# Six result buffers, x accumulated by DMA and the linear part on GpSimd in the spline stage of a convolution and spline kernel

## The reference

```python
out = relu(batchnorm(conv3x3(x, sign(w1)), gamma1, beta1))
out = batchnorm(conv3x3(out, sign(w2)), gamma2, beta2)
x = relu(out + x)                                   # input of the spline
u = (clip(a * x + b, -1.5, 1.5) + 1.0) * 0.5 * (K - 1)   # K = 32 cells
i = floor(u); t = clip(u - i, 0, 1)
i0, i1, i2, i3 = clip(i - 1), clip(i), clip(i + 1), clip(i + 2)      # to 0..K-1
spline = alpha[i0]*b0(t) + alpha[i1]*b1(t) + alpha[i2]*b2(t) + alpha[i3]*b3(t)   # cubic, R = 8
y_nl = einsum('bchwr,cr->bchw', spline, mix)
return id_gain * x + y_nl + bias
```

## Time and profile before

| | us |
|---|---|
| time before, median of 3 runs | 1254.49 (1253.94 to 1254.75) |
| the profiled execution, own time | 1254.66 |
| its span, first to last instruction | 1252.8 |
| first convolution and its norm | about 0 to 214 |
| second convolution and its norm | about 214 to 424 |
| spline, 32 chunks | 427 to 1253 |
| busy over the span | PE 1058.6, DVE 1062.8, ACT 868.8, POOL 113.4 |
| mean granted clock of PE | 0.926 of full speed |

### The profile page before, as it was taken

One profiled execution on the slowest core, in us unless ns is written; L12 is line 12 of the kernel. 1 busy time (PEld: TensorE's weight loads), 2 busy tenths in 40 slices (PEclk: granted clock), 3 DMA queues, 4 the chain that ended last, 5 costly groups with the idle time before them and its releaser, 6 DMA issues. The chain is left out here.

```text
span 1252.8 us, 51454 instructions
## 1 busy us (share of the span) xinstructions
PE 1058.6 (85%) x23562; PEld 710.2 (57%) x23562; DVE 1062.8 (85%) x951; ACT 868.8 (69%) x424; POOL 113.4 (9%) x189
## 2 busy tenths in 40 slices
PE   6999996999999368887888788878887888788876
PEld 4688885788888234554545455444544545455444
DVE  5765656766666689999999999999999999999987
ACT  4454544777787267688868877887788778877881
POOL 6000000282000000000000000000000000000000
PEclk9999998999999778998989889898998989889898
DMA  7666766576777386677767766777677667776552
GB/s 227 259 257 256 276 255 225 217 277 252 271 264 300 136 235 181 183 216 194 185 189 213 196 181 193 208 192 184 189 214 192 184 197 206 194 182 197 157 114 78
DMA packets 58215, 260.85 MB, mean 208 GB/s; under 512 B 16336, under 2 KB 16336, under 8 KB 50000
## 3 DMA queue, kind: packets, MB, share of 16 engines
q1 hardware_dynamic: 52528, 230.88, 56.3%
q0 software_dynamic: 4608, 25.69, 11.0%
q10 hardware_dynamic: 928, 1.90, 0.6%
HBM read 104.29 MB, written 77.07 MB: 145 GB/s over the span
## 5 line engine op out<-in xcount | busy, mean ns | idle before, releaser
L1181 PE MATMUL tab<-edge_mask,diag 128*32 128x392 bf16 x10240 | 501.8, 358 | 132.6 <-DVE poly L1090 130.8
L1181 PEld LDWEIGHTS tab<-edge_mask,diag 128*32 128x32 f16 x10240 | 281.7, 104 | 339.0 <-DVE poly L1090 143.4
L982 ACT ACTIVATE edge_mask<-cell,thr 128x6272 bf16<-128x6272 bf16 x62 | 338.5, 5508 | 0.0
L711 PE MATMUL acc<-split,w 64*64 64x392 f16 x4608 | 195.9, 329 | 12.0 <-DVE w L463 10.8
L711 PE MATMUL acc<-band_split,w 64*64 64x392 f16 x4608 | 197.9, 330 | 9.4 <-ACT band_split L368 7.2
L410 ACT ACTIVATE yout<-acc 128x1568 f32<-128x1568 f32 x64 | 94.2, 1473 | 160.6 <-PE acc L711 139.4
L1181 PE MATMUL tab<-middle_mask,diag 128*32 128x392 bf16 x4096 | 183.4, 332 | 25.0 <-DVE middle_mask L1052 25.0
L711 PEld LDWEIGHTS acc<-band_split,w 64*64 64x64 f16 x4608 | 164.1, 107 | 42.9 <-issue 14.1
L711 PEld LDWEIGHTS acc<-split,w 64*64 64x64 f16 x4608 | 155.3, 107 | 51.9 <-issue 12.6
L520 DVE BATCH_NORM_STATS2 stats<-yout 128x392 f32 (+1 forms) x240 | 118.0, 555 | 60.2 <-ACT yout L410 59.4
L930 ACT ACTIVATE zbuf<-lin,cst 128x1568 f32<-128x1568 f32 x32 | 54.3, 1697 | 163.8 <-DVE lin L1016 157.9
(11 more groups left out here) (126 smaller groups left out, 816.9 us busy)
## 6 DMA issues: line engine op xcount, KB each, us to landing
y_scratch<-yout SPq DMA_DIRECT2D x32, 1568.0 KB, 6.2
cell<-cell SPq DMA_DIRECT2D x496, 98.0 KB, 3.3
xin<-y_scratch SPq DMA_DIRECT2D x16, 1568.0 KB, 9.0
zbuf<-y_scratch SPq DMA_DIRECT2D x32, 784.0 KB, 5.9
lin<-in_x SPq DMA_DIRECT2D x32, 784.0 KB, 6.1
lin<-far POOLq DMA_DIRECT2D x32, 784.0 KB, 8.8
out<-lin SPq DMA_DIRECT2D x31, 784.0 KB, 4.1
xin<-in_x SPq DMA_DIRECT2D x15, 1568.0 KB, 9.3
```

The lines of the kernel that those rows point to most:

```text
L711: mm = pe.matmul(acc[h * C:(h + 1) * C, 2 * k + r, 0:TILE], weights[part][own, tap * C:(tap + 1) * C], image[own, first:first + ROWS, dx:d ...
L982: act.activation(mask_of(b, q)[:, :, :], cell4[b % 2][:, :, :], ACT.Sign, bias=thr[:, q:q + 1]).then_inc(sign_mask_ready, 1)
L1181: mm = pe.matmul(tab[(b + t) % 2][j * GROUP:(j + 1) * GROUP, sub, 0:SUB], keep["diag"][part][:, j % 2, t, q, :], mask_of(b, q)[:, j, sub * ...
```

## The change

- `lin` has six buffers instead of four. SP loads y2 (not x) straight into `lin` (`load`), four chunks ahead; chunks 0 and 1 are still loaded as before, in the convolutions' last round.
- ACT multiplies y in place (`scale`), and POOL issues a DMA that accumulates x onto it (`add_x`). Both stand three chunks ahead. `position` waits for that DMA (`x_added`) instead of for `total`, which is left for chunks 0 and 1 only.
- `linear` moves from DVE to POOL. POOL's queue is now, for each chunk, `linear(c + 2)`, `add_x(c + 3)`, `add_far(c)`.
- DVE multiplies `poly` by the offset twice (`times_offset`, from the integers) in place of `near_part`, `slope` and `add_slope`: square table, times offset, linear table, times offset. `distance_square` and `dist_sq` are gone. Because `slope` no longer writes `far_sq`, ACT's `far_square` waits for `far_part` of the chunk before.
- `finish(c - 1)` stands after `near_cube(c)`, where it stood ahead of it. On SP `store(c - 1)` stands after `spread(c + 2)`, where it stood first.
- All spline programs are written out for 32 chunks, without a loop.
- SP no longer waits for y2's stores ahead of the barrier; it does so in the spline, ahead of `load(2)`. The first ACT instruction is a square root (of a constant) instead of a copy.

```diff
-BUFS = 4
+LIN = 6
...
-            for b in range(2):
-                sp.wait_ge(stored[b], 32 * half_rounds)
...
-            act.activation(tmp[:, 5:6], row_scale[:, 0:1], ACT.Identity)
+            act.activation(tmp[:, 5:6], row_scale[:, 0:1], ACT.Sqrt)
...
-                wait_past(sp, offset_ready, before)
-                wait_past(sp, cell_ready, before)
-                sp.dma_start(place[b % 2][:, :], ysrc).then_inc(y_loaded[b % 2], 16)
-                wait_past(sp, stored[b % BUFS], free)
-                sp.dma_start(lin[b % BUFS][:, :], xsrc).then_inc(x_loaded[b % BUFS], 16)
...
+            def load(c):
+                wait_past(sp, stored[c % LIN], 16 * (c // LIN))
+                sp.dma_start(lin_of(c)[:, :], image_half(y2, c)).then_inc(y_loaded[c % LIN], 16)
...
-            def body(i, b, n):
-                if exists(n, b - 1):
-                    store(i, b - 1)
-                if exists(n, b + 3):
-                    load(i, b + 3)
-                if exists(n, b + 2):
-                    spread(i, b + 2)
...
+            spread(0)
+            for b in range(2):
+                sp.wait_ge(keep["y_stored"][b], 16 * PAIRS)
+            load(2)
+            spread(1)
+            load(3)
+            for c in range(CHUNKS):
+                if c + 4 < CHUNKS:
+                    load(c + 4)
+                if c + 2 < CHUNKS:
+                    spread(c + 2)
+                if c > 0:
+                    store(c - 1)
...
+            def linear(c):
+                pool.wait_ge(place_ready, c + 1)
+                pool.tensor_scalar(lin_of(c)[:, :], lin_of(c)[:, :], cc(NEG_B2),
+                                   par[:, ID_GAIN:ID_GAIN + 1], ALU.max, ALU.mult).then_inc(lin_ready, 1)
...
+            def add_x(c):
+                pool.wait_ge(scaled, c - 1)
+                pool.dma_start(lin_of(c)[:, :], image_half(x, c), accum_op=ALU.add).then_inc(x_added, 16)
...
+            linear(0)
+            linear(1)
+            add_x(2)
             for c in range(CHUNKS):
+                if c + 2 < CHUNKS:
+                    linear(c + 2)
+                if c + 3 < CHUNKS:
+                    add_x(c + 3)
                 add_far(c)
...
+            def scale(c):
+                act.wait_ge(y_loaded[c % LIN], 16 * (c // LIN + 1))
+                act.activation(lin_of(c)[:, :], lin_of(c)[:, :], ACT.Identity, scale=cc(BN2_S)).then_inc(scaled, 1)
...
+            def position(c):
+                if c < 2:
+                    act.wait_ge(sum_ready, c + 1)
+                else:
+                    act.wait_ge(x_added, 16 * (c - 1))
+                    act.wait_ge(offset_ready, c - 1)
+                    act.wait_ge(cell_ready, c - 1)
+                act.activation(place[c % 2][:, :], lin_of(c)[:, :], ACT.Identity, bias=cc(U_B),
                                scale=cc(U_S)).then_inc(place_ready, 1)
...
-                wait_past(act, slope_ready, 2 * c)
+                wait_past(act, far_part_ready, c)
...
-                c = BUFS * i + b
-                act.wait_ge(offset_ready, c + 1)
-                wait_past(act, near_ready, 2 * c)
-                act.activation(dist_sq[:, :], offset[b % 2][:, :], ACT.Square,
-                               scale=1 / POINT).then_inc(dist_sq_ready, 1)
...
-            def body(i, b, n):
-                following, after = exists(n, b + 1), exists(n, b + 2)
-                far_distance(i, b)
-                if after:
-                    position(i, b + 2)
-                far_square(i, b)
-                if after:
-                    cells(i, b + 2)
-                distance_square(i, b)
-                if following:
-                    distance(i, b + 1)
-                    edge(i, b + 1, EDGE_QUADS[0])
-                if following:
-                    edge(i, b + 1, EDGE_QUADS[1])
...
+            for c in range(2):
+                position(c)
+                cells(c)
+                spread(c)
+            distance(0)
+            scale(2)
+            for c in range(CHUNKS):
+                far_distance(c)
+                if c + 2 < CHUNKS:
+                    position(c + 2)
+                if c + 3 < CHUNKS:
+                    scale(c + 3)
+                far_square(c)
+                if c + 2 < CHUNKS:
+                    cells(c + 2)
+                if c + 1 < CHUNKS:
+                    distance(c + 1)
+                    for q in EDGE_QUADS:
+                        edge(c + 1, q)
...
-            def linear(i, b):
-                dve.wait_ge(place_ready, BUFS * i + b + 1)
-                dve.tensor_scalar(lin[b % BUFS][:, :], lin[b % BUFS][:, :], cc(NEG_B2),
-                                  par[:, ID_GAIN:ID_GAIN + 1], ALU.max, ALU.mult).then_inc(lin_ready, 1)
...
-            def near_part(i, b):
-                c = BUFS * i + b
-                dve.wait_ge(table_used, used(i, b, T_SQ))
-                dve.wait_ge(dist_sq_ready, c + 1)
-                dve.tensor_tensor(poly[b % 2][:, :], poly[b % 2][:, :], dist_sq[:, :], ALU.mult).then_inc(near_ready, 2)
...
-            def slope(i, b):
-                c = BUFS * i + b
-                dve.wait_ge(far_part_ready, 2 * c + 2)
-                dve.wait_ge(table_ready, used(i, b, T_LIN))
-                dve.scalar_tensor_tensor(out=quarters(far_sq), in0=summed(i, b, T_LIN), scalar=base(i, b, T_LIN),
-                                         in1=quarters(offset[b % 2]), op0=ALU.add, op1=ALU.mult).then_inc(table_used, 1)
...
-            def add_slope(i, b):
-                c = BUFS * i + b
-                dve.wait_ge(table_used, used(i, b, T_LIN))
-                dve.wait_ge(near_ready, 2 * c + 2)
-                dve.scalar_tensor_tensor(out=poly[b % 2][:, :], in0=far_sq[:, :], scalar=1 / POINT,
-                                         in1=poly[b % 2][:, :], op0=ALU.mult, op1=ALU.add).then_inc(slope_ready, 2)
...
+            def times_offset(c, t, done):
+                dve.wait_ge(table_used, used(c, t))
+                dve.scalar_tensor_tensor(out=poly[c % 2][:, :], in0=offset[c % 2][:, :], scalar=1 / POINT,
+                                         in1=poly[c % 2][:, :], op0=ALU.mult, op1=ALU.mult).then_inc(done, 1)
...
-            def body(i, b, n):
-                previous, following, after = exists(n, b - 1), exists(n, b + 1), exists(n, b + 2)
-                if previous:
-                    add_table(i, b - 1, T_VAL, slope_ready, 2 * (BUFS * i + b - 1) + 2)
-                    finish(i, b - 1)
-                if after:
-                    total(i, b + 2)
-                near_cube(i, b)
-                if after:
-                    fixed(i, b + 2)
-                    linear(i, b + 2)
-                far_cube(i, b)
-                far_part(i, b)
-                if following:
+            for c in range(CHUNKS):
+                if c > 0:
+                    add_table(c - 1, T_VAL, slope_ready, c)
+                if c + 2 < CHUNKS:
+                    fixed(c + 2)
+                near_cube(c)
+                if c > 0:
+                    finish(c - 1)
+                far_cube(c)
+                far_part(c)
+                if c + 1 < CHUNKS:
                     for q in MIDDLE_QUADS:
-                        middle(i, b + 1, q)
-                add_table(i, b, T_SQ, table_used, used(i, b, T_NEAR))
-                near_part(i, b)
-                slope(i, b)
-                add_slope(i, b)
-                if after:
-                    offsets(i, b + 2)
-            rounds(dve, body)
+                        middle(c + 1, q)
+                add_table(c, T_SQ, table_used, used(c, T_NEAR))
+                times_offset(c, T_SQ, near_ready)
+                add_table(c, T_LIN, near_ready, c + 1)
+                times_offset(c, T_LIN, slope_ready)
+                if c + 2 < CHUNKS:
+                    offsets(c + 2)
```

269 lines of the change are left out of this document (110 added, 159 removed).

## The result

| | before | after |
|---|---|---|
| time, median of 4 runs | 1254.61 us (1253.94 to 1254.75) | 1288.22 us (1286.73 to 1291.67) |
| ratio, 95% interval | | 1.0273 (1.0252 to 1.0294) |
| the profiled execution, own time and span | 1254.66, 1252.8 | 1291.67, 1289.8 |
| first and last `far_cube` | 459.44, 1233.89 | 468.03, 1271.06 |
| one chunk, mean of 31 | 24.98 | 25.90 |

The forecast was 1230 us, with a range from 1222 to 1266: wrong in sign. The account of the two profiled executions closes: 31 x (25.90 - 24.98) = 28.6 us in the chunks, 8.6 in a later first `far_cube`, -0.2 behind the last one, together 37.0 us of span. Against the forecast it closes too: 31 x (25.90 - 24.0) = 59.0, 2.9 for the first `far_cube` and -0.2 for the end are the 61.7 us between 1230 and 1291.67.

What follows compares the result with a forecast made beforehand. DVE, 97% busy, looked like the bound, with a loop through PE almost as long that would bind next at 24.0 us a chunk. 1254.66 - 0.7 - 2.3 + 8.7 - 30.4 = 1230 us, range 1222 to 1266.

Steps and rivals of the forecast that it cites:

- the paragraph on POOL: POOL's queue: `linear` estimated at about 4.0 us, issued with both DMAs well ahead of `far_part`, costing nothing if undisturbed.
- Rival 1: POOL's `linear` holds up DVE's `fixed`: cadence 24.8, total 1255 us, from 1246 to 1283; chance 0.34.
- the loop through PE: From `far_cube` through PE's value, near and far tables back to DVE: bounds 23.85 and 25.2 us, taken as 24.0.
- the opening: Spline's start: chunk 2's `position` waits for y, `scale` and x's accumulation in turn; first `far_cube` +8.7 us (5.8 to 12.0).
- DVE's instruction at 17.72: Trace row of 3.43 us, begun with POOL's running until 18.30 and not lengthened; read as speaking against POOL holding DVE.
- The row with 3.63: Trace row where a 0.36 us POOL instruction took 3.63 while DVE ran two instructions with two SBUF inputs.
- `position` at 15.85: On ACT, us after `far_cube`: 3.8 to `far_part`'s end, 8.8 for the DMA, 1.6 each for `far_distance` and `position`.
- slack against late landings: `far_cube` could come at 20.4 against a cadence of 24.0: 3.6 us slack, hiding far-part landings up to 12.4 us.
- DVE's work, 22.1 us: DVE's work per chunk: 24.91 less 1.76 for `total` and 1.0 for `linear`, three instructions replaced by three at 1.79.
- Fixed costs: Outside the chunks: table load -0.7, barrier before the spline -2.3 (0 to -3.1), longer start of the spline +8.7 us.
- Rival 2: Far part lands late behind two accumulating DMAs in POOL's queue: at 14 us, cadence 25.6, total 1280 us; chance 0.14.
- Rival 3: PE's clock as it was, value table 4.6 us on the mean: cadence 24.5, total 1245 us; chance 0.10.
- Rival 4: DVE's integer product 1 us slower for each `times_offset`: cadence 24.9 or more, about 1258 us; 0.04 together with others.

Runs made afterwards that it cites:

- e10: The changed kernel with POOL's `linear` doing only the maximum, without the multiplication by the gain (output not the reference's): 1254.26 us.
- e2: e1 plus the same `linear` instruction on POOL, on a spare tile that nobody reads or waits for: 1323.11 us.
- e4: The kernel before the change, with `linear` moved to POOL and nothing else changed: 1287.77 us.
- e8: The changed kernel with POOL's `linear` doing only 1120 of 1568 columns, the rest left undone: 1252.58 us.
- e1: The changed kernel with `linear` back on DVE, behind `finish`; POOL issues only its two DMAs: 1238.58 us, ratio 0.9868.
- e5: e1 with chunk 2 opened as before the change, y and x loaded apart and summed on DVE by `total`: 1231.6 us, ratio 0.9807.
- e6: e5 with the second of two middle masks on DVE moved behind the linear table: 1203.01 us, ratio 0.9580.
- e3: The changed kernel with POOL's `linear` cut into four instructions of 392 columns: 1265.55 us.
- e9: e6 with ACT's `position(c + 2)` ahead of `far_distance(c)` instead of behind it: 1191.24 us, ratio 0.9480.
- e11: The changed kernel with DVE's `fixed(c + 2)` moved behind `finish(c - 1)`, `linear` still on POOL: 1255.87 us, ratio 1.0003.

## Why the prediction was wrong, step by step

**The step that failed is in the paragraph on POOL:** "all are issued well ahead of `far_part`, so they cost nothing if POOL works undisturbed". POOL did work undisturbed. It was DVE that stood still, for 4.1 us a chunk in `fixed`, and that case had been put among the rivals, at 0.34. Of the 61.7 us between forecast and result, 52 are the cadence with and without `linear` on POOL, 31 x (25.90 - 24.23); 7 are the loop through PE, 31 x (24.23 - 24.0), and 3 the opening.

**The row that spoke against the rival could not speak about `fixed`.** DVE's instruction at 17.72 began with POOL's running until 18.30 and was "no longer than its like". It has two SBUF inputs and itself ends at 21.15. The runs show what such an instruction does: it ends 0.26 us behind the end of POOL's two-operation `linear` (0.7 behind a one-operation one in e10), or at its own time if that is later. An instruction that outlives POOL's by 2.85 us isn't lengthened under that rule. `fixed` is of another form, a TENSOR_SCALAR with one input, and is held until 0.83 behind POOL's end; on it the row says nothing, and I had counted it against the rival. The row with 3.63, in which POOL was held, was the informative one. By the Trainium skill, "SBUF — State Buffer", section "Who interferes with whom", the one that starts first keeps the other out for its whole instruction; for `fixed` (e2, and 26 of 26 chunks) and for POOL behind `fixed` or `times_offset` (6.44, 7.22) the traces agree. For DVE's instructions with two SBUF inputs they don't: a full block would put the end of `far_part` 1.85 us behind POOL's, and it lies 0.26 behind (e4). By the same section of the Trainium skill a DVE instruction with at most one SBUF input and outside the two-port modes doesn't contend, and the 1.83 to 1.85 us of `near_cube` and `far_cube` beside POOL agree.

**The term that was mis-sized is `linear`: 4.0 against 5.62 us.** The estimate scaled instructions with one operation to one with two. The first rival's sum with the right duration and with the same steps is 24.5 + 1.6 = 26.1 (25.90 measured), and 1254.66 + 5.7 + 31 x 1.1 = 1294 us for the whole (1291.67 in this execution). Its interval ended at 1283. With 4.1 to 4.3 us the runs e8 and e10 gave nearly its 1255. So its mechanism and working were right, and whether the result was "same" or "slower" hung on 1.6 us of one instruction. A gain of 24 us was out of reach at either duration.

**`position` at 15.85, slack against late landings.** It came at 15.6 to 16.85. The earliest are made not by the landing, which is what the sum was made of, but by ACT's own queue. `distance` waits for `finish`, the edge masks stand behind it, `far_distance` and `position` behind them. The prediction moved `finish` later and did not list that ACT's `distance` waits for it. In the changed kernel this closes the loop through POOL; in e1 DVE doesn't wait for it.

**The loop through PE: right.** With the hold gone (e1, e5) DVE waits for PE every chunk, at a cadence of 24.23 and 24.26 where 24.0 was taken; the distance from value to near table has a mean of 4.24 in e1 (27 chunks, 3.92 to 5.20), where the sum left 4.0 for it (24.0 - 9.13 - 10.9). That is 7 us of the total, had POOL cost nothing. e6 shows the loop itself. The lower bound that the near table sets by waiting for the linear table (3.8) is real: e6's distances are 3.71 or 3.72 in more than half of the chunks.

**DVE's work, 22.1 us: right.** 21.8 in the chunk shown. `times_offset` with its integer input takes what had been assumed:

```profile
L1070 DVE SCALAR_TENSOR_TENSOR poly<-offset,poly 128x1568 f32<-128x1568 int32 x64 | 114.7, 1792 | 2.2
```

**Late landing: small, but not hidden.** The far part's median is 8.5 us (5.8 to 15.0), like before. The prediction had landings up to 12.4 us hidden. In the loop that bound the changed kernel, ACT is ready for `far_distance` at 872.26, 8.4 us behind the issue at 863.87, so by this chunk a landing later than that already lengthens it, as in 13 chunks of the stretch. SP's order and the written-out programs show no wait of their own.

**Fixed costs.** The barrier's idle time fell from 3.08 to 0.98 us, where -2.3 had been taken, and the table load is gone. DVE at the spline's opening, as the earlier trace rows:

```profile
426.37 3.62 DVE L1006 SCALAR_TENSOR_TENSOR lin<-zbuf,cst,lin 128x1568 f32<-128x1568 f32 x2 [0.98 <-PEq L90]
...
465.14 1.10 DVE L1012 TENSOR_SCALAR zbuf<-zbuf,cst 128x1568 int32<-128x1568 f32 x1 [10.31 <-ACT zbuf L936]
466.15 1.85 DVE L1043 SCALAR_TENSOR_TENSOR poly<-tab,plain,poly 128x1568 f32<-128x1568 f32 x1
468.03 1.85 DVE L1050 SCALAR_TENSOR_TENSOR far<-tab,plain,far 128x1568 f32<-128x1568 f32 x1
```

It is later by 8.6 us where +5.7 had been summed. The path is the one described, scale, landing, `position`, `fixed`, `near_cube`; x's landing took 10.8 us where 8.8 had been taken. POOL's `linear` held `offsets` twice here, to 6.22 us each, beside this path: in e1, without it, the first `far_cube` comes no earlier (469.09).

**The verdict on the rivals.** Rival 1 happened, beyond its own upper end. Rival 2 can be made to happen (e3); here it cost a few tenths of a us a chunk. Rival 3, the value table slower than taken, is in e1's 24.23 in part. Rival 4 did not happen (1.79). The chance of 0.38 for "POOL costs DVE nothing" was the mistake.

## What to carry to other kernels

An instruction given to POOL isn't free for DVE even if nobody waits for its result: lay POOL's interval over DVE's timeline and price each DVE instruction under it by what it reads, and put POOL's work beside DVE's readers of PSUM or leave it on DVE, where it may take a fifth of the time. A duration is only scaled from rows with the same number of operations, and a row counts against a theory only if the theory would have made it look different. When two loops are almost equally long, look for a reordering of the shorter engine's queue that takes an instruction out of the other's loop: here that was worth more (e6 and e9, 40 us against e5) than all the work that was moved away (e5, 23 us in the medians).

## What the runs showed of the hardware

- With POOL's TENSOR_SCALAR running, DVE's TENSOR_SCALAR from SBUF to SBUF (`fixed`, `offsets`; 1.09 and 0.98 us alone) ends 0.83 us behind POOL's end in each chunk in which POOL started first, from whatever start. DVE's SCALAR_TENSOR_TENSOR with two SBUF inputs ends 0.26 behind it, or at its own time if that is later (`far_part` in e4 from 2.16 to 3.44, `finish` in e11 up to 5.78). The 0.26 goes with POOL's `linear` of 1568 columns and two operations: beside the one operation of e10 `finish` ends 0.7 behind (five chunks), beside the 1120 columns of e8 1.38 behind (one chunk). A wait for the whole instruction would have put that end 1.85 us behind; why it is less stays open. With one input in PSUM nothing is lengthened.
- It works the other way round as well: POOL starting 0.08 us behind `fixed` takes 6.44 instead of 5.62, behind `times_offset` 7.22.
- POOL's TENSOR_SCALAR on 128x1568 floats takes 5.62 us with two operations and 4.22 with one; DVE takes 1.09 with two.
- Two accumulating DMAs of 784 KB in POOL's queue: the second lands after 8.5 us (median) where they are issued 8 to 11 us apart (the changed kernel, e1), after 12.1 where 1.0 to 2.1 us apart (e3), but also after 11.1 where 8.4 us apart (e9). So the distance isn't the only cause; the other stays open.
- The profile counts a held instruction as busy. DVE showed 99% in the slower kernel and waits of almost nothing; only the duration of one instruction beside its like gives the hold away.
